# First layer: the shared expert of the second half right behind its scores, and the last collections behind the meeting

## What is computed

```python
def _L0_ffn_ref(X, routing_W, expert_bias, sW1, sb1, sW2, sb2, rW1, rb1, rW2, rb2):
    E = 8
    K = 2
    shared = jax.nn.silu(X @ sW1 + sb1) @ sW2 + sb2
    logits = jnp.einsum('btd,ed->bte', X, routing_W) + expert_bias
    activation = jnp.sqrt(jax.nn.softplus(logits))
    top_vals, top_idx = jax.lax.top_k(activation, K)
    combine = jnp.sum(jax.nn.one_hot(top_idx, E, dtype=X.dtype) * top_vals[..., None], axis=-2)
    hdn = jax.nn.silu(jnp.einsum('nd,edh->enh', Xf, rW1) + rb1[:, None, :])
    y = jnp.einsum('enh,ehd->end', hdn, rW2) + rb2[:, None, :]
    routed = jnp.einsum('ne,end->nd', cf, y).reshape(B, T, d)
    return shared + routed
...
x = x + _L0_ffn_ref(_layernorm(x, axis=-1), ...)
x = x + _L1_xattn_ref(_layernorm(x, axis=-1), ctx_1024, ctx_1024, ...)
x = x + _L1_ffn_ref(_layernorm(x, axis=-1), ...)
```

## Time and profile before

| | us |
|---|---|
| median of 3 runs (lowest, highest) | 918.27 (916.52, 922.88) |
| the profiled execution, time | 918.69 |
| the profiled execution, span from first to last instruction | 916.9 |
| mean granted TensorE clock | 0.949 |
| busy: PE, PEld | 792.0 (86%), 673.5 (73%) |
| busy: DVE, ACT, POOL | 538.0 (59%), 465.1 (51%), 420.7 (46%) |

### The profile page before, as it was taken

The page is one execution under the profiler, slowest core; times in us unless marked ns, Lnnn a source line. Parts: engine busy times, 40 slices in busy tenths (PEclk is TensorE's granted clock), DMA queues, the critical chain, the costliest instruction groups (busy, mean ns, idle before and its releaser), DMA issues.

```text
span 916.9 us, 16483 instructions
## 1 busy us (share of the span) xinstructions
PE 792.0 (86%) x4534; PEld 673.5 (73%) x4534; DVE 538.0 (59%) x1418; ACT 465.1 (51%) x1317; POOL 420.7 (46%) x382
## 2 busy tenths in 40 slices
PE   2989983999996789999998987688989999999991
PEld 1646643886785578989997876577968988889891
DVE  5847827552555489899998974466323333355452
ACT  1457642554565567777776677342313333333330
POOL 2200644554764388987453486414673222222221
PEclk9799996999999799999999997599999999999996
DMA  8899983886896933741802413412332222355424
GB/s 256 272 306 328 318 274 122 254 256 170 180 236 167 329 51 81 182 96 24 232 1 62 170 71 111 148 50 88 123 124 86 70 63 66 118 171 179 157 93 154
DMA packets 122018, 143.08 MB, mean 156 GB/s; under 512 B 10295, under 2 KB 113516, under 8 KB 120908
## 3 DMA queue, kind: packets, MB, share of 16 engines
q1 hardware_dynamic: 92056, 93.61, 34.2%
q0 software_dynamic: 19856, 38.95, 15.8%
q10 hardware_dynamic: 10022, 9.48, 3.3%
HBM read 71.28 MB, written 70.71 MB: 155 GB/s over the span
## 4 chain that ended last, share of the span: by engine, by line
PE 49%; DVE 15%; issue 8%; POOL 8%; ACT 7%; DMA 5%; DVEq 5%; SPq 1%; ACTq 0%; POOLq 0%
PE psum L653 25%; PE psum L1003 13%; POOL xs_dram L588 6%; ACT pr L1278 4%; PE psum L922 3%; DVE prl L1952 2%; DMA fx<-xs_dram 2%; DVE nmx L1937 2%; PE psum L942 2%; PE psum L1013 2%; DVEq L1943 2%; PE psum L832 2%; DVE sm L1942 2%; PE psum L990 1%; DMA X<-in_x_dram 1%
## 5 line engine op out<-in xcount | busy, mean ns | idle before, releaser
L608 POOL DMA_INDIRECT yk_dram<-ys,L x71 | 68.1, 959 | 203.3 <-ACT ys L1357 199.4
L2053 DVE TENSOR_TENSOR hs<-psum,hs 128x384 f32<-128x384 f32 x71 | 39.6, 558 | 166.1 <-PE psum L1003 134.4
L540 POOL DMA_INDIRECT X<-yl_dram,slots_y x64 | 101.6, 1587 | 37.3 <-issue 15.5
L1278 ACT ACTIVATE pr<-psum,nmx 128x64 f32<-128x64 f32 x512 | 108.0, 362 | 14.5 <-DVE nmx L1937 14.2
L1003 PE MATMUL psum<-whi,xTh 128*128 x284 | 103.7, 365 | 9.3 <-DVE xTl L2071 9.2
L515 POOL DMA_INDIRECT xs_dram<-N,slots x64 | 64.7, 1012 | 99.5 <-DVEq L1628 59.2
L653 PE MATMUL psum<-w_sb,cz 128*128 x426 | 104.9, 382 | 5.4 <-ACT ys L1357 5.4
L1003 PE MATMUL psum<-whi,xTl 128*128 x284 | 96.6, 340 | 0.0
L1003 PE MATMUL psum<-wlo,xTh 128*128 x284 | 96.3, 339 | 0.0
L582 POOL TENSOR_TENSOR pr<-pr,sm 128x1024 f32<-128x1024 f32 x32 | 62.3, 1945 | 70.9 <-DVE sm L1944 69.6
L653 PEld LDWEIGHTS psum<-w_sb,cz 128*128 128x128 f32 x426 | 75.5, 191 | 14.4 <-issue 7.0
(11 more groups left out here) (329 smaller groups left out, 1898.3 us busy)
## 6 DMA issues: line engine op xcount, KB each, us to landing
fx<-xs_dram SPq DMA_DIRECT2D x80, 130.0 KB, 3.9
xs_dram<-fill SPq DMA_DIRECT2D x4, 2600.0 KB, 16.9
yl_dram<-fy SPq DMA_DIRECT2D x80, 128.0 KB, 3.0
xs<-xs_dram SPq DMA_DIRECT2D x71, 130.0 KB, 2.1
wlo<-in_L_ffn_W_dram SPq DMA_DIRECT2D x4, 1536.0 KB, 12.4
ym<-yk_dram ACTq DMA_DIRECT2D x12, 512.0 KB, 5.2
xs_dram<-cz SPq DMA_DIRECT2D x1, 5200.0 KB, 26.1
xs_dram<-cz SPq DMA_DIRECT2D x8, 650.0 KB, 6.9
```

Of the source, the lines that this page charges most:

```text
L540: po.indirect_dma_start(X[:, t, :], None, YL[b // 2], bass.IndirectOffsetOnAxis(ap=slot_y[k][:, t:t + 1], axis=0), compute_op=ALU.add).the ...
L608: po.indirect_dma_start(YK, bass.IndirectOffsetOnAxis(ap=yid[:, j:j + 1], axis=0), ys[j % YB], None).then_inc(s[f"y_out{j % YB}"], 16)
L1278: last = act(pr[b][:, S * h:S * h + S], bank[2 * b + h // 8][:, S * (h % 8):S * (h % 8) + S], ACT.Exp, bias=nmx[:, h:h + 1])
L2053: tt(hs[j % 2], bank[4 + j % 2][:, 0:H1], hs[j % 2], ALU.mult).then_inc(s["e_hg"], 1)
```

## The change

Five edits. (1) On PE, ACT and (through its adds) DVE, shared(1) moves from between routed(0) and routed(1) to right behind scores(1); on PE it is ahead of ranks(1), on ACT ahead of softplus(1). Its second bank becomes 5 in place of 4, and its wait for `rout` goes. (2) ACT no longer loads the table of Ln ahead of scores(1). (3) The four adds of quads 0 to 3 move from the slots of half 0 into DVE's scores(1), one behind each quad's copy. (4) The four adds of quads 4 to 7 move from behind routed(0) and from the first slots of half 1 to where those of quads 0 to 3 were. (5) On POOL the last collection of half 0, (1, 1), moves from ahead of the meeting to behind the constants, ahead of the attention loop.

```diff
--- before.py
+++ after.py
@@ -550,9 +550,8 @@
             for g in range(LG):
                 send_rows(g)
             routed_done(0)
-            for b in range(2):
-                for k in range(2):
-                    collect(b, k, b * BT, b * BT + BT)
+            for b, k in ((0, 0), (0, 1), (1, 0)):
+                collect(b, k, b * BT, b * BT + BT)
             after(1)
             def numbers(v, k):
 
@@ -609,6 +608,7 @@
                     YK, bass.IndirectOffsetOnAxis(ap=yid[:, j:j + 1], axis=0),
                     ys[j % YB], None).then_inc(s[f"y_out{j % YB}"], 16)
 
+            collect(1, 1, BT, 2 * BT)
             routed_done(1)
             late = [(b, k, t) for b in (2, 3) for k in range(2) for t in range(b * BT, b * BT + BT)]
             for n in range(TILES):
@@ -801,12 +801,10 @@
             def shared_down(q):
 
                 pe.wait_ge(s["l_hs"], q + 1)
-                if q == LQ:
-                    pe.wait_ge(s["rout"], LG)
                 if q:
                     pe.wait_ge(s["l_ev"], 2 * q)
                 for t in range(QT):
-                    o = bank[(6, (5, 4)[q // LQ])[t // 2]][:, D * (t % 2):D * (t % 2) + D]
+                    o = bank[(6, 5)[t // 2]][:, D * (t % 2):D * (t % 2) + D]
                     mm(o, hsh[q % 2][:, t * P:t * P + P], sw2_sb[:, :], True, False)
                     last = mm(o, ones_r, b2p[:, E, :], False, True)
                 last.then_inc(s["l_sy"], 1)
@@ -876,9 +874,9 @@
                 fold(j)
             shared(0)
             scores(1)
+            shared(1)
             ranks(1)
             routed(0)
-            shared(1)
             routed(1)
             meet()
 
@@ -1171,7 +1169,7 @@
                         ac.wait_ge(s["l_xu"], q - LQ + 1)
                     elif q == 2:
                         ac.wait_ge(s["st_out00"], 16 * len(range(0, PAIRS, DEEP)))
-                    for h, k in enumerate((6, (5, 4)[g])):
+                    for h, k in enumerate((6, 5)):
                         act(ysh[q % LQ][:, 512 * h:512 * h + 512], bank[k], ACT.Copy).then_inc(s["l_ev"], 1)
 
             def split_high(k, m, v):
@@ -1227,12 +1225,11 @@
                 fold(j)
             table(1, ACT.Silu)
             shared(0)
-            table(2, ACT.Ln)
             scores(1)
+            shared(1)
             softplus(1)
             table(1, ACT.Silu)
             routed(0)
-            shared(1)
             routed(1)
             meet()
 
@@ -1555,6 +1552,8 @@
                     if q + 1 < q0 + LQ:
                         rows_in(q + 1)
                     turned(q)
+                    if g:
+                        shared_add(q - LQ)
                     if g == 0:
                         if q % 2:
                             ve.wait_ge(s[f"s_in{2 + q // 2}"], 16 * 4)
@@ -1649,9 +1648,7 @@
                     nc.vector.tensor_copy(fxT[j % 2].rearrange("p c n -> p (c n)"), bank[j % 2][:, 0:D]).then_inc(s["f_xt"], 1)
                     i = j - LS * g - 3
                     if g == 0 and i >= 0 and i % 6 == 0 and i < 6 * LQ:
-                        shared_add(i // 6)
-                    if g and j - LS * g in (1, 3):
-                        shared_add(LQ + 2 + (j - LS * g) // 2)
+                        shared_add(LQ + i // 6)
                     i = j - LS * g - 8
                     if g and i >= 0 and i % 4 == 0 and i < 32:
                         m, v = i // 4 % 4, i // 16
@@ -1735,8 +1732,6 @@
             scores(1)
             choose(1)
             routed(0)
-            shared_add(LQ)
-            shared_add(LQ + 1)
             routed(1)
             routed_norm(0, 0)
             routed_norm(0, 1)
```

## The result

| | us |
|---|---|
| before, beside the first runs of the change | 918.53 (916.52 to 922.88, 4 runs) |
| changed, first | 928.46 (925.12 to 930.11, 4 runs), ratio 1.0102, 95% interval 1.0058 to 1.0146 |
| before, beside the second | 918.62 (913.51 to 927.01, 25 runs) |
| changed, second | 924.66 (921.9 to 929.94, 8 runs), ratio 1.0059, 95% interval 1.0022 to 1.0096 |
| spans of the two profiles of the changed kernel | 925.2 and 924.7 |

The change makes the kernel slower, by 0.6 to 1.0%. The first median lies almost on the forecast of 928.5; the second shows that this was luck in part: about 6 us is the better value, not 10. Medians in this document are over all runs; one run of the kernel before (930.03, among the 35 beside the first four experiments) was in a slower state, and the ratios leave it out.

What follows compares the result with a forecast made beforehand. It took the chain as mostly PE, with serial waits on DVE, SP's loads and POOL. On the 916.9 us span, 3.3 + 5.0 + 1.4 + 0.5 = plus 10.2 gave 927.1, 928.5 on the median; 8-in-10 range 920 to 934.

Steps and rivals of the forecast that it cites:

- Scores, shared(1), ranks: PE from scores(1) to slots: scores 0.8 us shorter, shared(1) ahead of ranks(1) makes the slots start 11.1 us later.
- Softplus: ACT behind shared(1): two table loads of 1.28 us, done at 157.4, hidden by `places` with 1.5 us to spare.
- Slots of half 0: PE's 40 slots of half 0: same length as before, ending at 224.2, 11.1 us later.
- Shared(1) gone, the wait for the first load: Between the halves on PE: minus 17.1 us of shared(1), plus a new 8.9 us wait for the load behind vraw.
- Rival A: Between the halves: first load lands in 2.3 us, gap 3.8, PE's clock doesn't fall; 922.4 us, chance 0.14.
- Restart and slots of half 1: PE in half 1: cold start plus 1.0 us, less interference from collections minus 0.6 us.
- Rival B: Slots of half 1 get faster, pace 1.26 us where it was 1.51, so not slower: 918.3 us, chance 0.07.
- Start of the attention: Behind the meeting: POOL's collections delay scale(0) by 5.0 us, DVE's wait adds 1.4, PE's low clock 0.5.
- Rival C: Start of the attention absorbs POOL's delay, only plus 3.3 us stays: 921.6 us, chance 0.15.
- rival D: Attention start loses more: collections land in 8.1 us, low clock holds through logits(2); 931.0 us, chance 0.12.
- The sum: Whole kernel: all terms together plus 10.2 us, a span of 927.1, or 928.5 on the median; chance 0.52.
- Up to the meeting: From scores(1) to POOL's meeting behind half 1: plus 2.9, plus 1.0, minus 0.6, together plus 3.3 us.

Runs made afterwards that it cites:

- the first four experiments: Changed kernel with collection (1, 1) back ahead of the meeting, 918.85; kernel before with only that collection moved, 922.71; changed with vraw behind six slot loads, 923.9; changed with one slot-load stream, 919.28.
- both runs of the collection alone: Changed kernel with collection (1, 1) back ahead of the meeting, 918.85 us; kernel before with only that collection moved behind the meeting, 922.71 us.
- the three with one stream: Changed kernel with both halves' slot loads as one SP stream, 919.28; also collection (1, 1) ahead of the meeting, 912.72; also shared(1) split around ranks(1), 906.95.

## Why the prediction was right, and where it was not

The direction, the class of mechanism and the range held: 928.46 and 924.66 lie within 920 to 934. The chance for slower by over 1% was put at 0.52 and that for within 1% at 0.43; the first set of runs gives 1.02%, the second 0.59%, so the truth is more likely the second case. (By its own terms the first chance is 0.12 + 0.39 = 0.51.) Step by step, forecast against the mean of two profiles each:

- *Scores, shared(1), ranks:* plus 11.1 forecast, plus 10.8 measured. Scores(1) took 13.6 us where it took 14.5, so 0.9 for the 0.8 forecast. The first up stands 42.0 us behind the start of scores(1), forecast 42.3. Softplus was hidden, and its two table loads cost the 1.28 us of the rows each, with no further gap.
- *Slots of half 0:* 0 forecast, minus 0.5 measured, within the spread of one profile.
- *Shared(1) gone, the wait for the first load:* minus 8.2 forecast, minus 10.5 measured. This is the term that was mis-sized. The wait was forecast at 8.9 us and is 6.4 to 6.6. The mechanism is right (a load behind vraw, issued 1.4 us behind PE's end; moving vraw halves the wait, moving both removes it), but vraw took 5.0 us to land, where I took 7.3 from its one row of before. That was no chance of one execution: with shared(1) gone from there it lands in 5.0 to 5.2 us in all five profiles, with shared(1) beside it in 7.3, 6.0 and 6.0. A landing time was carried from one arrangement into another. Rival A (3.8) was as far off as the forecast. The section of the Trainium skill that the prediction cites beside this term (DMA: Bandwidth & Descriptors, Anatomy of one DMA) is on DMAs that GpSimd issues, and these loads are SP's; the estimate from it comes to a gap of 3.8 us, not 3.6, and the sum did not rest on it.
- *Restart and slots of half 1:* plus 0.4 forecast, minus 0.6 measured. From the first transpose to the fifth it was 238.91 - 233.49 = 5.42 us, against 5.33 of before: the low clock came (0.77 over 234 to 240) but no more than what was saved there, probably the two adds; the two weren't separated. Rival B's pace did not come: 58.4 and 56.8 against 58.3 and 58.1.
- *Start of the attention:* plus 6.9 forecast, plus 6.6 measured, the step that decided the sign. It is a sum of misses that cancel. scale(0) starts behind the eight collections, 317.32 - 298.23 = 19.1 us from the start of the constants, where I had 20.3, mostly since it starts 1.0 us behind the start of the last collection and not 1.9; so plus 3.8 for 5.0, and 0.6 more because this scale takes 2.50 us and not 1.90. DVE's wait was longer than forecast (the last collection landed in 8.5 us, not 6.5). At the first values matmul the delay is 8.0 us in the first profile and 7.2 in the second, over the 6.9 forecast. From there to the experts some 1.1 us come back, where I had written that nothing does. Rival C falls with both runs of the collection alone; rival D's late landing came, and its time did not.
- *The sum:* plus 10.2 forecast, plus 5.8 in the stages. Up to the meeting I had plus 3.3, and the stages give minus 0.8: this is where the forecast was wrong. The first set's plus 9.9 is 4 more; its profile had a late beginning (126.8 for 122.3), and whether its other runs had it too isn't known.

What I had right in kind was that a hole on one engine is there because something else is serial: 17 us of work went in, and 10.8 us of new hole came out behind it.

## What to carry to other kernels

Before work is moved into an idle stretch, look at what ends that stretch: here a chain between DVE and PE ran through it, and the moved work belongs between its links, not ahead of one (put ahead of ranks(1), it delays the slots by 10.8 us; split around it, by 5.4). Work taken away from between two stages uncovers whatever was quietly prefetched under it, so move the prefetch first. And a queue that waits anyway (POOL at the meeting, 12 us) is the cheapest place for its work; behind the wait the same instructions lie on the path. A short wait on PE costs more than itself where the granted clock falls behind it: the 5.16 us ahead of ranks(1) cost another 1.6.

## What the hardware showed unexpectedly

The beginning of the kernel, the same program in all variants but for the places of later code, ended anywhere from 120.4 to 126.8 us. It goes with the granted PE clock of 40 to 60 us, without an exception in the twelve profiles: 1.00 in the five that end at 120.4 to 120.8 us, 0.94 to 0.97 in the four at 121.9 to 122.3, 0.90 in the two at 124.5 and 124.7, and 0.77 in the one at 126.8, the first of the changed kernel. In the first profiles of both kernels it is 0.95 before and 0.77 after:

```profile
40.00:60.00 20.00, 16.18 (x62) 9.87 (x60) 7.02 (x23) 13.42 (x21) 0.00 (x0) 0.95 1.03 315
```

```profile
40.00:60.00 20.00, 19.11 (x61) 11.15 (x59) 3.96 (x13) 10.46 (x18) 0.00 (x0) 0.77 1.09 320
```

What makes the one or the other, and whether the clock is cause or consequence, wasn't settled. The spread is as large as the effect that was to be measured, and it is why the stages were compared and not the spans.

The same load of 1 MB (vraw) took 5.0 to 5.2 us to land in the five profiles in which it is issued ahead of the slot loads with shared(1) moved away. It took 6.0 to 7.3 in the three in which PE does shared(1) meanwhile, 7.5 behind six slot loads, and 7.5 to 8.0 in the three with one stream. What decides it wasn't tested.
